# Score rounds paired at the ends of each attention, and a new order of work in a step of a two-layer transformer kernel

## The reference, cut to what matters

```python
q, k, v = qkv[:, :, 0], qkv[:, :, 1], qkv[:, :, 2]
attn = softmax(einsum('bnhd,bmhd->bhnm', q, k) * SCALE)
x = x + gate_sa * (einsum('bhnm,bmhd->bnhd', attn, v).reshape(...) @ sa_proj_w + sa_proj_b)
...   # cross attention the same way, keys and values from the context
x = x + gate_ff * (gelu(xm3 @ fc1_w + fc1_b) @ fc2_w + fc2_b)
```

## Time and profile before

| | |
|---|---|
| median of 3 runs | 1804.01 us |
| profiled execution, its own time | 1797.43 us |
| its span from first to last instruction | 1795.6 us |
| TensorE busy | 1594.9 us (89%) |
| VectorE busy | 1117.6 us (62%) |
| ScalarE busy | 972.2 us (54%) |
| GpSimd (POOL) busy | 720.3 us (40%) |
| mean granted TensorE clock | 0.959 |

### The profile page before, as it was taken

The page is one execution under the profiler, slowest core; times in us unless marked ns, Lnnn a source line. Parts: engine busy times, 40 slices in busy tenths (PEclk is TensorE's granted clock), DMA queues, the critical chain, the costliest instruction groups (busy, mean ns, idle before and its releaser), DMA issues.

```text
span 1795.6 us, 45329 instructions
## 1 busy us (share of the span) xinstructions
PE 1594.9 (89%) x17760; PEld 1372.3 (76%) x17760; DVE 1117.6 (62%) x2628; ACT 972.2 (54%) x2009; POOL 720.3 (40%) x983
## 2 busy tenths in 40 slices
PE   5779989899898989999897998989989898998977
PEld 4657878778787877878786787877878787787866
DVE  3446666566665665666666766676666666666554
ACT  2445465555546655465664555656455554545533
POOL 1232323224232332333645546454454535546321
PEclk8879999999999999999999999999999999999989
DMA  6010010100101010011110100000000000000000
GB/s 221 13 38 14 26 37 10 53 8 20 37 26 37 11 53 5 23 37 37 43 37 30 37 13 25 10 28 5 10 25 14 25 7 19 14 13 14 2 13 13
DMA packets 33968, 49.43 MB, mean 28 GB/s; under 512 B 3456, under 2 KB 24896, under 8 KB 33760
## 3 DMA queue, kind: packets, MB, share of 16 engines
q1 hardware_dynamic: 33760, 46.54, 8.2%
HBM read 38.07 MB, written 8.45 MB: 26 GB/s over the span
## 4 chain that ended last, share of the span: by engine, by line
PE 74%; DVE 8%; ACT 8%; issue 6%; POOL 3%; DMA 1%; SPq 0%; DVEq 0%; ACTq 0%; POOLq 0%
PE score L606 9%; PE p_unit L687 8%; PE score_t L626 7%; PE p_unit L500 6%; PE p_mix L662 5%; PE p_unit L501 5%; PE p_unit L502 5%; PE p_out L500 3%; PE p_out L502 3%; PE p_out L501 3%; DVE neg_max L1045 3%; PE p_turn L670 2%; PE p_mix L533 2%; PE p_turn L677 2%; PE p_turn L651 2%
## 5 line engine op out<-in xcount | busy, mean ns | idle before, releaser
L1045 DVE TENSOR_REDUCE neg_max<-score 128x4 f32<-128x512 f32 x512 | 330.1, 687 | 264.1 <-PE score L606 262.5
L606 PE MATMUL score<-k_t,q_t 32*128 32x256 f32 x2048 | 303.9, 416 | 65.5 <-POOL q_t L1293 30.8
L626 PE MATMUL score_t<-q_less,k_t 32*128 32x128 f32 x4096 | 307.0, 289 | 0.8 <-ACT probs_t L914 0.8
L606 PEld LDWEIGHTS score<-k_t,q_t 32*128 32x128 f32 x2048 | 190.2, 194 | 110.7 <-issue 61.7
L626 PEld LDWEIGHTS score_t<-q_less,k_t 32*128 32x128 f32 x4096 | 257.1, 192 | 13.3 <-issue 9.2
L914 ACT ACTIVATE probs_t<-score_t 128x512 f32<-128x512 f32 x384 | 209.1, 598 | 106.2 <-PE score_t L626 105.8
L1246 POOL TENSOR_TENSOR xt_lo<-xt,xt_hi 128x256 fp32r<-128x256 f32 x128 | 94.8, 740 | 395.8 <-ACT xt_hi L838 395.8
L833 ACT ACTIVATE xt<-p_mix,mod_now 128x128 f32<-128x128 f32 x384 | 155.2, 456 | 138.0 <-PE p_mix L533 135.3
L687 PE MATMUL p_unit<-w_out,heads_t 128*128 128x256 f32 x512 | 144.3, 404 | 42.8 <-ACT heads_t L927 15.8
L1091 DVE CAST hid_hi<-hid 128x256 fp32r<-128x256 f32 x256 | 102.0, 398 | 81.6 <-ACT hid L900 80.8
L500 PE MATMUL p_out<-w_hi,hid_lo 128*128 128x256 f32 x512 | 149.1, 291 | 1.5 <-DVE hid_lo L1093 0.3
(11 more groups left out here) (144 smaller groups left out, 4149.8 us busy)
## 6 DMA issues: line engine op xcount, KB each, us to landing
ctxt<-in_ctxT SPq DMA_DIRECT2D x16, 512.0 KB, 3.9
side<-gates SPq DMA_DIRECT2D x15, 512.0 KB, 4.8
x_new<-in_x SPq DMA_DIRECT2D x32, 128.0 KB, 2.0
x_mid<-xs SPq DMA_DIRECT2D x8, 512.0 KB, 3.3
x_new<-x_mid SPq DMA_DIRECT2D x32, 128.0 KB, 2.0
out<-xs SPq DMA_DIRECT2D x8, 512.0 KB, 2.9
k_t<-in_L_f_wT SPq DMA_DIRECT2D x2, 1024.0 KB, 5.3
k_t<-in_ln_wT SPq DMA_DIRECT2D x2, 512.0 KB, 7.9
```

What stands on the lines that cost most here:

```text
L606: mm = pe.matmul(score[r % 2][:, t * 2 * N:(t + 1) * 2 * N].rearrange("p (e n) -> p e n", e=2), q_t[s][rows(r), t, tokens], k_t[s][rows(r) ...
L626: mm = pe.matmul(score_t[r % 2][:, x * N:(x + 1) * N], k_t[s][rows(r), t, e, tokens], q_less[rows(r), j % 2, t, e, :], start=True, stop=True)
L1045: dve.tensor_reduce(by_half[:, :, 2 * r:2 * r + 2, 0], score[r % 2][:].rearrange("p (t e n) -> p t e n", t=CT, e=2), AX.X, ALU.max, negate ...
```

## The change

1. Scores of batch 0 are made in both rounds in one step (step 1 of an attention instead of steps 0 and 1), in four banks: its second round writes `score_t`. Turned scores of batch 3 are made in both rounds in one step (step 9 instead of 9 and 10), its second round in `score`. Waits follow.
2. The order of kinds of work in a step is new on TensorE, ScalarE, VectorE and POOL.
3. New steps for units, for the first LayerNorm, for the MLP units (steps 36 to 43, so that the last step of a group is 45 and not 47), KEYS_LAG, AT_CTX, AT_MASK, MOD_AT.

```diff
-KEYS_LAG = 4
-FIRST_STATS, FIRST_Z, FIRST_LNT = -13, -9, -9
-AT_CTX = -6
-AT_MASK = 15
-MOD_AT = (-15, -5, 12)
-UNIT_AT = {-6: ("k", SELF, 0), -5: ("q", SELF, 0), -3: ("k", SELF, 1), 1: ("q", SELF, 1), 2: ("v", SELF, 0), 4: ("v", SELF, 1),
+KEYS_LAG = 3
+FIRST_STATS, FIRST_Z, FIRST_LNT = -13, -11, -10
+AT_CTX = -5
+AT_MASK = 8
+MOD_AT = (-15, -7, 22)
+UNIT_AT = {-6: ("k", SELF, 0), -3: ("q", SELF, 0), -1: ("k", SELF, 1), 2: ("q", SELF, 1), 3: ("v", SELF, 0), 4: ("v", SELF, 1),
            6: ("k", CROSS, 0), 7: ("v", CROSS, 0), 11: ("k", CROSS, 1), 14: ("q", CROSS, 0), 16: ("v", CROSS, 1), 18: ("q", CROSS, 1)}
...
-for _step, _n in zip(range(MLP_FROM, MLP_FROM + 10), (0, 10, 1, 1, 6, 12, 1, 0, 0, 1)):
+for _step, _n in zip(range(MLP_FROM, MLP_FROM + 8), (2, 4, 1, 6, 3, 9, 4, 3)):
...
-def round_at(step, lag):
+def score_at(step):
     for s, start in enumerate(START):
-        if 0 <= step - start - lag < 2 * GB:
-            b, h = divmod(step - start - lag, 2)
-            yield s, b, h
+        for b, h in itertools.product(range(GB), range(2)):
+            if step == start + max(2 * b + h, 1):
+                yield s, b, h
+def turned_score_at(step):
+    for s, start in enumerate(START):
+        for b, h in itertools.product(range(GB), range(2)):
+            if step == start + AT_EXP + min(2 * b + h, 2 * GB - 2):
+                yield s, b, h
...
-PE_ORDER = ("round", "proj", "mlp", "max", "mix", "turn", "norm", "first", "unit", "back")
+PE_ORDER = ("round", "max", "mix", "proj", "norm", "mlp", "turn", "unit", "back", "first")
...
-        up_ring = score + score_t
+        up_ring = score_t + score
+        def score_bank(b, r):
+            return (score_t if b == 0 and r >= 2 else score)[r % 2]
+        def turned_bank(b, r):
+            return (score if b == GB - 1 and r >= 2 else score_t)[r % 2]
...
-                if group == 0 and j == 0 and h == 0:
-                    pe.wait_ge(gates_made, 1)
+                if group == 0 and j == 0:
+                    pe.wait_ge(gates_made if h == 0 else bias_added, 1)
+                elif b == 0:
+                    pe.wait_ge(exps_made, group * 32 + 4 * j)
                 else:
-                    pe.wait_ge(max_made, group * 32 + 4 * j + 2 * h)
+                    pe.wait_ge(max_made, group * 32 + 4 * j + 2 * h - (2 if b == 1 and h == 0 else 0))
...
-                if group == 0 and j == 0 and h == 0:
-                    pe.wait_ge(bias_added, 1)
-                else:
+                if 0 < b + h and (b < GB - 1 or h == 0):
                     pe.wait_ge(exps_made, group * 32 + 4 * j + 2 * h)
```

More of the change, by code:

```diff
@@ L600, in scores @@
                         mask = mask_row[rows(r), tokens].unsqueeze(1).broadcast_to([32, SLOTS, N])
-                        pe.matmul(score[r % 2][:].rearrange("p (x n) -> p x n", x=SLOTS), ones_row[rows(r), :], mask,
+                        pe.matmul(score_bank(b, r)[:].rearrange("p (x n) -> p x n", x=SLOTS), ones_row[rows(r), :], mask,
                                   start=True, stop=False, skip_group_check=True)
@@ L634, in score_round @@
                 for group, step in live(t):
-                    for s, b, h in round_at(step, 0):
+                    for s, b, h in score_at(step):
                         products = scores(group, s, b, h)
@@ L697, in up @@
                     pe.wait_ge(w_new_lo, 3)
[L698 to L701, removed]
+                if u < HID_SLOTS:
+                    pe.wait_ge(exps_made, (group + 1) * 32 + (16 if group < GROUPS - 1 else 0) - (2 if u < 2 else 0))
                 else:
@@ L742, in body @@
                     for group, step in live(t):
+                        for s, b in batch_at(step, AT_TURN_MAX):
+                            turn_max(group, 4 * s + b)
+                    for group, step in live(t):
+                        for s, b in batch_at(step, AT_MIX):
+                            mix_values(group, s, b)
+                    for group, step in live(t):
                         for s, b in batch_at(step, AT_PROJ):
                             project(group, s, b)
+                    for group, step in live(t):
+                        for s, b in batch_at(step, AT_LNT):
+                            turn_z(group, s + 1, b)
                     for group, step in live(t):
@@ L772, in body @@
                             turn_back(group, 4 * s + b)
+                    for group, step in live(t):
+                        for b in first_at(step, FIRST_LNT):
+                            turn_z(group, 0, b)
             def modulation(chunks, bank, at):
@@ L958, in body @@
                     for group, step in live(t):
-                        if layer_of(group) == 1 and step in KEYS_AT:
-                            low_keys(group, KEYS_AT[step])
+                        for s, b, h in turned_score_at(step):
+                            exps(group, s, b, 2 * h)
+                            exps(group, s, b, 2 * h + 1)
                     for group, step in live(t):
@@ L1151, in body @@
                     for group, step in live(t):
+                        if layer_of(group) == 1 and UNIT_AT.get(step - DVE_SWAP, "v")[0] != "v":
+                            swap(group, UNIT_AT[step - DVE_SWAP])
+                    for group, step in live(t):
                         if layer_of(group) == 0 and UNIT_AT.get(step - DVE_KEYS, "v")[0] == "k":
@@ L1154, in body @@
                     for group, step in live(t):
-                        for s, b, h in round_at(step, 0):
+                        for s, b, h in score_at(step):
                             row_max(group, s, b, 2 * h)
                             row_max(group, s, b, 2 * h + 1)
-                    for group, step in live(t):
-                        for s, b in batch_at(step, AT_PROJ + DVE_OUT):
-                            take_output(group, 4 * s + b)
                     for group, step in live(t):
@@ L1166, in body @@
                             less_max(group, s, b)
+                    for group, step in live(t):
+                        for s, b in batch_at(step, AT_PROJ + DVE_OUT):
+                            take_output(group, 4 * s + b)
+                    for group, step in live(t):
+                        for what, n in HIDDEN_AT.get(step, ()):
+                            if what == "split":
+                                split_hidden(group, n)
+                            else:
+                                take_hidden_output(group, n)
                     for group, step in live(t):
@@ L1174, in body @@
                             make_masks(group)
-                    for group, step in live(t):
-                        if layer_of(group) == 1 and UNIT_AT.get(step - DVE_SWAP, "v")[0] != "v":
-                            swap(group, UNIT_AT[step - DVE_SWAP])
-                    for group, step in live(t):
-                        for what, n in HIDDEN_AT.get(step, ()):
-                            if what == "split":
-                                split_hidden(group, n)
-                            else:
-                                take_hidden_output(group, n)
             dve.memset(ones_row[:], 1.0).then_inc(ready, 1)
@@ L1313, in body @@
                     for group, step in live(t):
+                        if step == AT_CTX:
+                            split_ctx(group)
+                    for group, step in live(t):
                         for k, b in normed_at(step, AT_LNT + ACT_MOD, FIRST_LNT + ACT_MOD):
@@ L1318, in body @@
                             add_hidden_output(group, b)
-                    for group, step in live(t):
-                        if step == AT_CTX:
-                            split_ctx(group)
             def low_weights(c):
```

39 lines of the change are left out of this document (13 added, 26 removed).

## The result

The changed kernel takes 1751.11 us (median of 4 runs, 1749.17 to 1751.56) against 1802.3 us for the kernel before beside it: a ratio of 0.9716, interval 0.9689 to 0.9743, so 51 us faster. Forecast were 1745 us, 59 us less, range 1700 to 1795. The profiled execution took 1751.56 us, span 1749.7, against a forecast of 1738: between the two profiled executions, from which the sum was worked out, the gain is 45.9 us and not 59. Of all runs named here one, of e5_serial_wait (1822.5 us), was in a slower state and is left out of its median and ratio.

The account below looks back on a forecast made before the run. TensorE, busy 1594.9 of 1795.6 us, was taken as the bound; gains summing to 59 us took the profiled execution from 1797 to 1738 us, hence a forecast of 1745 us for the median, range 1700 to 1795.

Parts of the forecast that it names:

- 49 round times go: Pairing rounds in each attention removes 49 round times of 1.05 us from TensorE: 51 us, 3.15 per period.
- Rival E: Two score rounds at once do not overlap as the mixed pair does: 34 us come back, 1779 us; chance 0.08.
- The maxima are just covered: VectorE's four maxima after step 1's double round hide behind TensorE work; uncovered, up to 1.4 us per attention, 44 in all.
- rival B: Evacuation gives the gain back, as each double round waits for its four maxima: 44 us, 1789 us; chance 0.10.
- Term (a): Step 20's round waits for queries made in step 18: TensorE idle 3.0 us in layer 0, 4.7 in layer 1.
- Term (b): Step 21 holds only a round, and the next needs its maxima: 1.4 us idle in layer 0, 1.2 in layer 1.
- What the new steps take away: Wait for the second key copy goes, about 1.9 us a layer 0 period; back-to-back norms' wait, 1.0 us a period.
- The change of layer: Where layer 0 ends, group 9's context load gets four steps instead of two: 6 us gained (0 to 8).
- the sum: Layer 0 gives 29 us, layer 1 20, the 49th round 1, layer change 6, last group 3: together 59 us.
- rival C: Thinned steps 19 to 22 bring the lower clock: 4.7 us in 16 groups, 75 us, 1820 us; chance 0.10.
- (c): TensorE's other waits, behind heads_t, at steps 15, 4 and 19 and small ones, stay as they are, 0.4 to 1.2 us.
- Rival D: Waits fold better than counted and clock losses shrink: 2.5 us more in 16 groups, 1705 us; chance 0.17.

Follow-up runs that it names:

- e5_serial_wait: Changed kernel, but the second round of each of the 64 double rounds waits until the first has ended: 1809.6 us, 1.0038 of before.
- e2: Kernel before with the paired rounds alone, order of work and all other steps as before: 1747.4 us, 0.9718 of before.
- e6: Changed kernel, but ScalarE moves the unit ahead of modulating in the four steps of a group's first norm: 1752.9 us, 0.9727 of before.
- e7: Changed kernel, but VectorE makes the second key copy of step 21 behind the row maxima: 1744.5 us, 0.9687 of before.
- e3: Changed kernel without the pairing: single rounds and MLP units as before, new order and other new steps kept: 1811.4 us, 1.0081 of before.
- e4: Changed kernel with the second half of the cross values made in step 19 and not 16: 1717.1 us, 0.9545 of before.
- e8: Changed kernel with 12 unused transposes added at the end of step 19 and 8 at the end of step 21: 1727.5 us, 0.9587 of before.
- e10: Kernel before with the paired rounds alone, and second half of cross values in step 19, not 16: 1783.2 us, 0.9913 of before.
- e1: Changed kernel with the two rounds of each double round issued one behind the other, not interleaved: 1766.9 us, 0.9823 of before.

## Why the prediction was right, and where it was not

1. "49 round times go", 51 of the 59 us: right. Busy fell by 53.7 us with about as much time at the lower clock as before (147 and 154 us), the double rounds take 1.08 and 1.10 us, e5 gives back 58 us when they can't overlap, and e2 has the gain from the pairs. Rival E is out.
2. "The maxima are just covered": half right. Under the new order the cost is 0.8 us per self attention (12.7 us, as the turning of the maxima waits for scale_heads behind four maxima); under the old order 1.6 us a group, 25 us, over half of rival B's 44. So rival B's mechanism is real, and smaller than what the pairs save.
3. Term (a), the round of step 20: right in size. Layer 1 waits 4.2 us a group in seven groups and 7.0 at the change of layer (36.6 in all, forecast 4.7 each), layer 0 1.06 + 1.60 = 2.7 us (forecast 3.0). Its cause was only partly ScalarE: e6 shows that in layer 1 POOL's queue holds the same place.
4. Term (b), step 22: 1.4 to 2.2 us in layer 0 (forecast 1.4), 1.3 to 1.8 in layer 1 (forecast 1.2). The working left out the key copy (1.0 us) that stands ahead of the maxima in step 21 of layer 0; e7 agrees in direction, but is not clear of noise.
5. "What the new steps take away": k_t fell from 18.5 to 5.4 us and the norm's wait from 17.6 to 2.0, as forecast. The change of layer did not give its 6 us: the wait for the context is gone, but one of 7.0 us for the rotated queries stands in its place. The working looked at ScalarE's and TensorE's waits there and not at what stands in VectorE's and POOL's queues. The period that holds the change fell from 115.0 to 109.6 us (between GELU table loads), 5.4 us, of which 3.15 are the rounds.
6. The step that failed inside a right total is the sum's treatment of everything but the rounds, 8 us of gain on paper: it puts the change of the clock at nothing, and the new order and steps at 0.5 us a period less idle in layer 0, 0.6 more in layer 1 and a few us at the change of layer and the end. By itself the new order costs 14 us (e3), mostly clock, and beside the pairs it is worth nothing (0.9716 against e2's 0.9718). Layer 0 was to give 3.65 us a period and gave 1.1 (7.5 / 7): the lower level holds 8% of it and not 2%, some 44 us more, of which busy time shows 11 us of cost, and idle is 9.6 us a period where 8.5 were forecast. Idle waits that the sum lacks are those of turn_max (12.7 us) and of the projection for heads_t (29.5 us, 15.8 before). The prediction had the clock as rival C at 75 us net loss and a chance of 0.10; it happened in layer 0, inside the forecast, at less than a third of its size.
7. Part of the total is luck. The start gave 16.3 us, of which 5 are round times. Busy fell by 10.6 us there and idle by 5.6, and the sum has next to nothing for either beyond the rounds. In layer 1 two errors cancel: over the five full periods behind 1119.09 busy fell by 4.4 us each where the sum has 3.15, and idle rose by 2.2 where it has 0.6. The start's surplus makes up for about half of what layer 0 and the change of layer lack (18 and 6 us), so the total came within 8 us of 59 by the medians, 13 by the profiled executions, while sections were up to 18 us off.

A slip in the working of (c) is without weight: its waits add up to 4.4 us a period, and 4.1 and 3.8 are used.

Rival D's mechanism happened in part: the projection's waits for the moves of its bank (26.2 us before: q_t, side and v_pad at L687) are gone, but those for heads_t nearly doubled, and idle as a whole is 7.8 us up. What stays open is why the start gained more than its rounds. It isn't the clock by itself: in e6 the start's clock is 0.97 and in the changed kernel 0.91, and both starts take as long (171.99 and 171.45 us). The pairs alone give 14.8 us there (e2), the new order alone 4.9 (e3); no run isolates more. Open, too, is why the new order costs clock: e4, e8 and e10 show that the clock falls behind short waits and that filling them keeps it up, but no run takes the order apart kind by kind.

## What to carry to other kernels

Count the steps in which work truly runs alone before pricing a merge: here 49, not 64. Then work out what else the change does to each engine's queue, POOL's too: here 8 us of gain were forecast for it, and it lost 14 by itself. Price a thinned stretch by the granted clock behind it as well as by its waits, and when the engine must wait anyway, put real work there, but look at what that work covered where it stood. Moving one engine's stage ahead helps only if no other in-order queue holds the same result.

## What the runs showed of the hardware

Work that computes nothing made the kernel faster: 20 transposes per group, 2.2 us, took 23 us off 1751, as they filled waits and the granted clock rose from 0.956 to 0.980. The lower clock came behind waits as short as 1 to 2 us (1.06 and 1.60 in the changed kernel, 1.46 in e10). And TensorE overlaps matmuls of different row groups over some depth even when they are issued one round behind the other (e1): four score products per round overlapped fully (1.08 us for a pair, as interleaved), eight turned ones half (1.65 us, against 1.10 interleaved and 2.34 with a wait between).
